# Expert feed-forward blocks: weights stationary, tokens moving, unrolled blocks

## The reference, cut to what matters

```python
logits = x @ router_w + router_b                 # x: layer-normed tokens, 2048 x 256; 8 experts
top_v, top_i = jax.lax.top_k(softmax(logits), 2)
weights = zeros((T, E)).at[arange(T)[:, None], top_i].set(top_v / sum(top_v))
gate = einsum('td,edi->eti', x, gate_w) + gate_b[:, None, :]      # i: 512 FF units
up   = einsum('td,edi->eti', x, up_w) + up_b[:, None, :]
h = silu(gate) * up
expert_out = einsum('eti,eid->etd', h, down_w) + down_b[:, None, :]
y = einsum('te,etd->td', weights, expert_out)                     # then t + y
```

## Time and profile before

| | us |
|---|---|
| median of three runs | 454.5 |
| span of the profiled execution, first to last instruction | 453.7 |
| runs, lowest and highest | 454.16, 454.62 |
| PE, DVE, POOL, ACT busy | 346.5, 343.3, 288.8, 209.2 |
| expert stage, first to last issue of L1146 (`weigh`) | 254.2 to 444.1 |

### The profile page before, as it was taken

How to read it: one execution, slowest core, us unless ns; L and a number is a source line. 1 busy time by engine, 2 the same in 40 slices (tenths; PEclk the granted TensorE clock), 3 DMA queues, 4 the chain that set the end, 5 groups by cost and what they waited for, 6 DMA issues and landing times.

```text
span 453.7 us, 13159 instructions
## 1 busy us (share of the span) xinstructions
PE 346.5 (76%) x4491; PEld 214.4 (47%) x4492; DVE 343.3 (76%) x693; ACT 209.2 (46%) x343; POOL 288.8 (64%) x459
## 2 busy tenths in 40 slices
PE   0078677767866766697259998999999999999971
PEld 0077434444444454542023654656566566565540
DVE  6988799799899999877882776666776776677650
ACT  1047637755956857645501433334434434433430
POOL 5616456666666666644585367777877878788651
PEclk9997568668668668689569999999999999999995
DMA  8410002322322222507764132333233333323322
GB/s 197 123 36 1 2 2 96 95 94 97 95 92 92 92 95 94 144 2 194 219 248 139 25 48 46 48 56 58 46 56 55 51 49 55 58 46 58 56 25 23
DMA packets 24960, 35.27 MB, mean 78 GB/s; under 512 B 4992, under 2 KB 18304, under 8 KB 24160
## 3 DMA queue, kind: packets, MB, share of 16 engines
q1 hardware_dynamic: 16256, 24.46, 17.5%
q0 software_dynamic: 7488, 10.23, 14.1%
q10 hardware_dynamic: 1184, 0.14, 0.2%
HBM read 25.39 MB, written 9.44 MB: 77 GB/s over the span
## 4 chain that ended last, share of the span: by engine, by line
PE 25%; DVE 23%; issue 19%; POOL 13%; DMA 9%; ACT 5%; DVEq 2%; POOLq 1%; SPq 1%; ACTq 0%
PE bank L881 6%; DMA w_stage<-token_rows,q_hi 5%; POOL w_stage L513 4%; PE bank L902 3%; POOL small L509 3%; DVE att L1348 2%; PE bank L549 2%; DVE s_exp L1314 2%; DVE v_exp L1367 2%; PE bank L777 2%; DVE q_exp L1382 2%; POOL v_exp L488 2%; PE bank L664 2%; DVE maxes L1307 2%; DMA token_rows<-z_stack 1%
## 5 line engine op out<-in xcount | busy, mean ns | idle before, releaser
L881 PE MATMUL bank<-w_exp,w_stage 128*128 x468 | 113.7, 380 | 1.3 <-issue 0.2
L526 POOL DMA_INDIRECT out_dram<-w_stage,q_hi x39 | 62.4, 1600 | 16.9 <-issue 16.9
L881 PEld LDWEIGHTS bank<-w_exp,w_stage 128*128 128x128 f16 x468 | 45.6, 97 | 41.8 <-issue 4.6
L408 POOL TENSOR_TENSOR w_exp<-w_stage,w_exp 128x1024 f16<-128x1024 f32 (+1 forms) x24 | 51.0, 2129 | 22.4 <-ACT w_exp L1041 22.4
L902 PE MATMUL bank<-w_exp,q_exp 128*128 x468 | 58.6, 276 | 2.1 <-DVE q_exp L1587 2.1
L513 POOL DMA_INDIRECT w_stage<-token_rows,q_hi x39 | 48.1, 1234 | 6.0 <-issue 6.0
L1570 DVE TENSOR_TENSOR v_exp<-bank,x_rows 128x512 f32<-128x512 f32 x39 | 27.0, 692 | 32.9 <-PE bank L881 32.8
L1146 ACT ACTIVATE w_stage<-w_stage,gate 128x256 f32<-128x256 f32 x39 | 19.8, 508 | 68.2 <-DVE w_stage L1592 68.2
L902 PEld LDWEIGHTS bank<-w_exp,q_exp 128*128 128x128 f16 x468 | 43.0, 98 | 11.8 <-issue 5.4
L1127 ACT ACTIVATE w_stage<-bank 128x256 f16<-128x256 f32 x39 | 14.9, 383 | 52.9 <-PE bank L869 52.9
L1587 DVE TENSOR_TENSOR q_exp<-bank,q_exp 128x512 f16<-128x512 f32 x39 | 27.0, 692 | 10.2 <-ACT q_exp L1138 10.0
(11 more groups left out here) (253 smaller groups left out, 814.2 us busy)
## 6 DMA issues: line engine op xcount, KB each, us to landing
w_stage<-in_L_ffn_gate_w_dram SPq DMA_DIRECT2D x8, 512.0 KB, 3.5
w_stage<-in_L_ffn_up_w_dram SPq DMA_DIRECT2D x8, 512.0 KB, 3.5
w_stage<-in_L_ffn_down_w_dram SPq DMA_DIRECT2D x8, 512.0 KB, 3.5
x_rows<-in_x_dram SPq DMA_DIRECT2D x8, 256.0 KB, 6.1
out_dram<-x_rows SPq DMA_DIRECT2D x4, 512.0 KB, 6.0
token_rows<-z_stack SPq DMA_DIRECT2D x4, 512.0 KB, 6.0
x_rows<-in_L_ffn_gate_b_dram SPq DMA_DIRECT2D x1, 2048.0 KB, 11.6
z_stack<-in_L_ffn_up_b_dram SPq DMA_DIRECT2D x2, 1024.0 KB, 6.8
```

What stands on the lines that cost most here:

```text
L408: pool.tensor_tensor(lo, w_stage[:, k, :], hi, ALU.subtract).then_inc(s["w_lo_done"], 1)
L526: pool.indirect_dma_start(out, bass.IndirectOffsetOnAxis(s_idx[par], 0), yw[par], None, compute_op=ALU.add).then_inc(s["y_scattered"], 16)
L881: mm = pe.matmul(GU[par][k][:], xs[par][:, c, :], w_exp[:, w * W_EXP + k * W_PIECE + c * FF:][:, bass.ds(e, FF)], start=(n == 0), stop=(n ...
```

## The change

`hidden` swaps its operands: for each of 4 chunks of 128 FF units and 2 chunks of channels, a 128x128 piece of `w_exp` is stationary and the 128 tokens move, 24 matmuls for gate and 24 for up. The result has FF units on partitions, which is the layout `down` needs, so `hidden_turned` goes. The biases become one value per partition in a new tile `b_cols`, filled in the first stage by two small DMAs, one transpose on TensorE and one copy on VectorE; the 4 MB broadcast loads go. `silu` takes the gate bias inside the activation, straight from PSUM, in four pieces of 128 columns; `gated` adds the up bias and multiplies in one instruction for each of four pieces. All blocks are written out instead of looped. GpSimd uses the table columns as index operands, without copies and holds, and the order of gathers and scatters, of the two hidden halves, and of the work on VectorE and ScalarE is as below.

```diff
-                pool.tensor_copy(g_idx[par], t_gather[:, bass.ds(b, 1)]).then_inc(s["gcol_ready"], 1)
-                pool.wait_ge(s["gcol_ready"], b + 1)
-                pool.tensor_tensor(hold[1], one_word, one_word, ALU.mult)
-                pool.indirect_dma_start(xg[par], None, token_rows, bass.IndirectOffsetOnAxis(g_idx[par], 0))\
+            def gather(b):
+                if b >= 2:
                     pool.wait_ge(s["xt_ps"], b - 1)
+                pool.indirect_dma_start(xg[b % 2], None, token_rows,
+                                        bass.IndirectOffsetOnAxis(t_gather[:, b:b + 1], 0))\
+                    .then_inc(s[f"x_got{b % 2}"], 16)
+            def scatter(b):
+                if b >= 1:
                     pool.wait_ge(s["y_scattered"], 16 * b)
                 pool.wait_ge(s["y_ready"], b + 1)
...
-            gather(0, 0, first=True)
-            gather(0, 1, first=True)
-            gather(1, 0)
-            gather(1, 1)
-            scatter(0, 0, first=True)
-            with pool.Fori(0, 2 * BODY - 1) as i:
-                gather(i + 2, 0)
-                scatter(2 * i + 1, 1)
-                gather(i + 2, 1)
-                scatter(2 * i + 2, 0)
+            gather(0)
+            gather(1)
+            for b in range(BLOCKS):
+                if b + 2 < BLOCKS:
+                    gather(b + 2)
+                scatter(b)
...
-                for xs, w in ((x_hi, 0), (x_hi, 1), (x_lo, 0)):
+                for f in range(FF_CHUNKS):
                     for c in range(2):
-                        mm = pe.matmul(GU[par][k][:], xs[par][:, c, :],
-                                       w_exp[:, w * W_EXP + k * W_PIECE + c * FF:][:, bass.ds(e, FF)],
-                                       start=(n == 0), stop=(n == 5))
+                        for xs, w in ((x_hi, 0), (x_lo, 0), (x_hi, 1)):
+                            mm = pe.matmul(GU[b % 2][k][:, P * f:P * f + P],
+                                           w_exp[:, w * W_EXP + k * W_PIECE + c * FF + P * f:][:, bass.ds(e, P)],
+                                           xs[b % 2][:, c, :], start=(c == 0 and xs is x_hi and w == 0),
+                                           stop=(c == 1 and w == 1))
...
+            for b in range(BLOCKS):                  # TensorE
+                if b + 1 < BLOCKS:
+                    e = weights_of(b + 1)
+                    hidden(b + 1, 0, e)
+                    hidden(b + 1, 1, e)
+                e = weights_of(b)
+                if b + 2 < BLOCKS:
+                    load_expert(b + 2)
+                    tokens_in(b + 2)
+                down(b, e)
...
+            for b in range(BLOCKS):                  # ScalarE
+                if b >= 1:
+                    weigh(b - 1)
+                if b + 1 < BLOCKS:
+                    silu(b + 1)
+                if b + 2 < BLOCKS:
+                    tokens_high(b + 2)
+                if b + 1 < BLOCKS:
+                    hidden_high(b + 1)
...
+            for b in range(BLOCKS):                  # VectorE
+                if b >= 1:
+                    down_bias(b - 1)
+                if b + 1 < BLOCKS:
+                    gated(b + 1)
+                if b + 2 < BLOCKS:
+                    tokens_low(b + 2)
+                if b + 1 < BLOCKS:
+                    hidden_low(b + 1)
```

More of the change, by code:

```diff
@@ L895, in down @@
-            def down(b, par, e, first=False):
+                        for xs, w in ((x_hi, 0), (x_lo, 0), (x_hi, 1)):
[3 more added lines that the diff above has]
+                                           stop=(c == 1 and w == 1))
+                mm.then_inc(s["gate_ps"] if k == 0 else s["up_ps"], 1)
@@ L896, in down @@
+            def down(b, e):
                 pe.wait_ge(s["hl_ready"], b + 1)
-                if not first:
+                if b >= 1:
                     pe.wait_ge(s["yadd_ready"], b)
                 n = 0
-                for c in range(4):
+                for c in range(FF_CHUNKS):
                     for hs, w in ((h_hi, 0), (h_lo, 0), (h_hi, 1)):
-                        mm = pe.matmul(YB[:, 0:L_COL], hs[par][:, c, :],
+                        mm = pe.matmul(YB[:, 0:L_COL], hs[b % 2][:, c, :],
@@ L906, in down @@
                 mm.then_inc(s["y_ps"], 1)
[L908 to L921, removed]
             pe.wait_ge(s["tables_ready"], 1)
-            load_expert(0, 0)
-            load_expert(1, 1)
-            tokens_in(0, 0, first=True)
+            load_expert(0)
+            load_expert(1)
+            tokens_in(0)
             keep_warm(4)
[L928 to L939, removed]
+            e = weights_of(0)
+            hidden(0, 0, e)
+            tokens_in(1)
+            hidden(0, 1, e)
+            for b in range(BLOCKS):
[8 more added lines that the diff above has]
+                down(b, e)
         @block.scalar
@@ L1128, in tokens_high, with silu @@
                                ACT.Copy).then_inc(s["xh_ready"], 1)
-            def silu(b, par, first=False):
-                act.wait_ge(s["gadd_ready"], b + 1)
-                if not first:
-                    act.wait_ge(s["h_ready"], b - 1)
-                act.activation(g_silu[par], g_sum[par], ACT.Silu).then_inc(s["silu_ready"], 1)
-            def hidden_high(b, par, first=False):
-                act.wait_ge(s["ht_ps"], b + 1)
-                act.activation(h_hi[par], bank[5][:].rearrange("p (c t) -> p c t", c=4),
+            def silu(b):
+                e = act.value_load(t_expert[0:1, b:b + 1], min_val=0, max_val=EXPERTS - 1)
+                if b >= 2:
+                    act.wait_ge(s["h_ready"], FF_CHUNKS * (b - 1))
+                act.wait_ge(s["gate_ps"], b + 1)
+                for f in range(FF_CHUNKS):
+                    act.activation(g_silu[b % 2][:, P * f:P * f + P], bank[2 * (b % 2)][:, P * f:P * f + P], ACT.Silu,
+                                   bias=b_cols[:, bass.ds(e * FF_CHUNKS + f, 1)]).then_inc(s["silu_ready"], 1)
@@ L1139, in hidden_high, with weigh @@
+            def hidden_high(b):
+                act.wait_ge(s["h_ready"], FF_CHUNKS * (b + 1))
+                if b >= 2:
+                    act.wait_ge(s["y_ps"], b - 1)
+                act.activation(h_hi[b % 2], h_sb[b % 2].rearrange("p (c t) -> p c t", c=FF_CHUNKS),
                                ACT.Copy).then_inc(s["hh_ready"], 1)
-            def weigh(b, par, first=False):
+            def weigh(b):
                 act.wait_ge(s["yadd_ready"], b + 1)
-                if not first:
-                    act.wait_ge(s["scol_ready"], b)
-                act.activation(yw[par], y_sum[par], ACT.Copy, scale=t_weight[:, bass.ds(b, 1)])\
+                if b >= 2:
+                    act.wait_ge(s["y_scattered"], 16 * (b - 1))
+                act.activation(yw[b % 2], y_sum[b % 2], ACT.Copy, scale=t_weight[:, b:b + 1])\
@@ L1147, in weigh @@
                     .then_inc(s["y_ready"], 1)
-            def act_block(b, par, first=False, more=2):
-                hidden_high(b, par, first=first)
-                if more >= 1:
-                    silu(b + 1, 1 - par, first=first)
-                if more >= 2:
-                    tokens_high(b + 2, par)
-                weigh(b, par, first=first)
-            tokens_high(0, 0, first=True)
-            tokens_high(1, 1, first=True)
-            silu(0, 0, first=True)
-            act_block(0, 0, first=True)
@@ L1161, in _ @@
-            with act.Fori(0, BODY) as i:
-                for k in range(4):
-                    act_block(4 * i + k + 1, (k + 1) % 2)
-            act_block(BLOCKS - 2, 1, more=1)
-            act_block(BLOCKS - 1, 0, more=0)
+            tokens_high(0)
+            silu(0)
+            tokens_high(1)
+            hidden_high(0)
+            for b in range(BLOCKS):
+                if b >= 1:
+                    weigh(b - 1)
[5 more added lines that the diff above has]
+                    hidden_high(b + 1)
@@ L1168, in _ @@
+            weigh(BLOCKS - 1)
         @block.vector
@@ L1586, in hidden_low, with down_bias @@
+            def hidden_low(b):
                 dve.wait_ge(s["hh_ready"], b + 1)
[L1587 removed]
+                if b >= 2:
+                    dve.wait_ge(s["y_ps"], b - 1)
+                dve.tensor_tensor(h_lo[b % 2], h_sb[b % 2].rearrange("p (c t) -> p c t", c=FF_CHUNKS), h_hi[b % 2],
                                   ALU.subtract).then_inc(s["hl_ready"], 1)
[L1590 removed]
+            def down_bias(b):
+                e = expert_of(b)
@@ L1608, in _ @@
-            tokens_low(0, 0)
-            tokens_low(1, 1)
-            e0 = expert_of(0)
-            dve.wait_ge(s["bias_rows"], 32)
-            gate_bias(0, 0, e0, first=True)
-            dve.wait_ge(s["up_rows"], 32)
-            up_bias(0, 0, e0)
-            gated(0, 0, first=True)
-            dve_block(0, 0, first=True)
-            with dve.Fori(0, BODY) as i:
-                for k in range(4):
-                    dve_block(4 * i + k + 1, (k + 1) % 2)
```

(11 more changed lines are left out.)

150 lines of the change are left out of this document (48 added, 102 removed).

## The result

The kernel after takes 631.72 us (median of 4 runs, 630.16 to 632.44), the kernel before beside it 454.56 us (4 runs): a ratio of 1.390, 95% interval 1.387 to 1.393, slower. Forecast were 612 us, and 568 to 644.

What follows compares the result with a forecast made beforehand. The bound was taken to be a circle of waits for one block through gather and scatter: 0.5 + 1.7 + 3.5 + 2.4 + 1.0 = 9.1 us, 9.4 with cold downs; 36 rounds plus head and tail gave 612 us, range 568 to 644.

Steps and rivals of the forecast that it cites:

- The step that carried it: GpSimd's queue: gather b+2 stands behind scatter b-1, which waits for down(b-1), so rounds go from 5.01 to 9.4 us.
- circle for one block: Down(b-1), weigh, scatter b-1, gather b+2, token transposes, down(b) wait on each other in turn: 9.1 us warm, 9.9 cold.
- a: End of weigh to start of the scatter: 0.83 us before, taken 0.5 without the hold, bounds 0.3 and 0.83.
- b: Start of scatter to start of gather: 2.27 us before, taken 1.7 without copy and hold, bounds 1.6 and 2.27.
- c: Start of gather to start of the token transposes, landing included: taken 3.5 us, bounds 2.8 and 3.9.
- d: Start of the token transposes to start of down_bias: taken 2.4 us warm, 3.2 cold, bounds 2.04 and 3.3.
- e: Start of down_bias to end of weigh: 1.08 us before, taken 1.0, bounds 0.95 and 1.08.
- the mechanism: TensorE's clock falls in the round's pause of about 3 us; some 4 in 10 downs run cold, round 9.4 us.
- My first rival: Gather on time, TensorE's sequencer bounds: 40 register operations at 0.12 us plus about 1.0, round 5.9, total 487 us; chance 0.09.
- P: The time of one round of the expert stage, the circle's length: taken 9.4 us, from 8.2 to 10.3.
- Edits taken at nothing: Edits around the rounds, such as small bias loads, dropping the 4 MB of broadcasts and unrolled code: each taken as 0.
- The forecast rival of 436 us: Faster than before: TensorE's array bounds the round at 4.5 us, total 436 us; chance 0.06.

Runs made afterwards that it cites:

- e1: The kernel after with one edit: GpSimd issues gather b+3 ahead of scatter b again, as before the change; 505.66 us, 1.116 of before.
- e2: The kernel before with one edit: scatter b stands ahead of gather b+3, holds and copies kept; 646.12 us, 1.427 of before.
- e4: As e1, but TensorE reads expert 0's weights at a fixed address for every block, without address operations; 451.65 us, 0.997 of before.
- e3: The kernel after with six unused 512-column matmuls between hidden and the token transposes of each round; 604.36 us.
- e5: The kernel before with table columns as indices, no copies or holds, GpSimd's blocks written out, gather b+3 still ahead of scatter b; 447.92 us, 0.988 of before.
- e6: As e1, but only down reads expert 0's weights at a fixed address, 8 register operations fewer; 506.86 us, 1.118 of before.
- e7: As e1, but only the gate half of hidden reads expert 0's weights at a fixed address, 16 operations fewer; 456.41 us, 1.004 of before.
- e8: As e5, without the 4 MB of broadcast bias loads, so the additions read other data; 448.79 us, 0.986 of before.

## Why the prediction was right

**The step that carried it held.** That gather b+2 now stands behind scatter b-1, and that this makes a circle for one block, is shown from both sides: e1 takes it out of the new kernel (-126 us), e2 puts it into the old one (+193 us). It is shown without the operands, the layout or the unrolling, so the swapped matmuls are not what the 177 us are mainly about. The 51 us that e1 leaves are about the price of the addresses: e4 takes 54 us off e1.

**The terms of the round.** Means over the 36 rounds of the profile after, beside the forecast (warm is a round at 2.4 GHz, cold one at 1.2):

| term | forecast | measured | |
|---|---|---|---|
| a, weigh to scatter | 0.5 | 0.80 | the hold went, but 0.75 of "issue" stayed |
| b, scatter to gather | 1.7 | 1.89 | 1.59 and 0.30 |
| c, gather to token transposes | 3.5 | 3.08 | the landing fell from 3.2 to 2.8 |
| d, transposes to down_bias | 2.4 warm, 3.2 cold; 2.72 mixed | 3.00 | from 2.2 (warm) to 3.4 (cold) |
| e, down_bias to the end of weigh | 1.0 | 0.97 | |
| round | 9.4 | 9.73 | 12 us in 36 rounds |

Three terms came out longer than forecast (a by 0.30, b by 0.19, d by 0.28) and c shorter by 0.42. The sum is off by 0.34 only because these partly cancel, which is luck. Why the landing fell is not isolated; it is 2.8 in the three kernels with the circle for one block (after, e2, e3) and 2.9 to 3.2 in those with the gather ahead (before, e1, e5, e6, e7). In a, I took away the hold's 0.18 and a part of the pause behind it; the pause was not the hold's. Where the scatter waits for `weigh`, a measures 0.80 in every kernel here without the hold, against 0.83 to 0.85 with it (before, e2), so the hold was worth next to nothing there; what the direct columns saved lies in b (2.27 to 1.89).

**The clock.** I let 4 in 10 downs be cold, from two pauses of before. In the profile after, 28 of the first 37 lie above 2.6 us in term d, three in four, and the mean granted clock of the stage is 0.82. So the mechanism was right and its share was put too low. Behind a pause of 3.10 us the level was 0.50, that is 1.2 GHz (the stretch from 384.40 above); behind the 1.29 us that e3 leaves it was 2.4 GHz. The pauses run from 2.5 to 4.7 us, and the length of one pause does not say alone what the next down takes: in the timeline above, the one of 3.73 us was followed by a down of 1.84, the one of 2.71 by a down of 2.76. What decides within the round stays open. The Trainium skill ("TensorE: Matmul & The Clock Gate", Why this matters for your kernels) warns of idle gaps of about this length between bursts; as a warning this agrees with the trace, but not as a limit, since here the cold down came behind the shorter pause. e3 gives the price in this kernel, 27 us.

**TensorE's sequencer.** The trace of before showed the operations 0.12 us apart, and hidden was put at 4.0 us. The spacing holds: its median is 0.124 to 0.125 us in the kernels before and after and in every run here that has such operations. Hidden itself takes 2.9 to 4.4 us in the kernel after, 3.7 on average, and as forecast costs nothing there, as it is covered by the pause. My first rival (487 us if the gather were on time) came within 19 us of the 505.7 of e1, but partly by luck: it adds down's 8 operations to hidden's 32, and e6 shows that down's cost nothing, while the rest of the round beside hidden's operations is 2.2 us and not 1.0. Two traces show how it goes. First e1, one round (L1509 is `tokens_low`, for whose result the next hidden waits):

```profile
355.89 0.41 PE L836 MATMUL bank<-ident,w_stage 128*128 128x128 f32 x2 [0.35 <-issue]
356.23 1.48 PE L861 MATMUL bank<-w_exp,q_exp 128*128 x12
356.92 0.42 DVE L1509 TENSOR_TENSOR w_stage<-bank,w_stage 128x256 f16<-128x256 f32 x1
357.54 4.26 PE L848 MATMUL bank<-w_stage,w_exp 128*128 128x128 f16 x48
```

In 34 rounds of e1 the first address operation of hidden came 0.04 to 0.11 us behind the end of L1509. So the operations stand behind hidden's wait for the new tokens, and the 1.45 us from the start of the transposes to the end of L1509 are spent whatever down does: down's operations and matmuls lie beside them. The round of e1 is these 1.45 us, the 32 operations of 4.1 us, and some 0.7 from the last of them to the next transposes. In the kernel after a cold down gives them a head start, because the tokens are ready before down ends:

```profile
316.30 0.42 DVE L1509 TENSOR_TENSOR w_stage<-bank,w_stage 128x256 f16<-128x256 f32 x1 [3.75 <-ACT w_stage L1073]
...
L848 PEldq FUSED_REGOPS  x32: 46/46/46, 316.8 to 320.9; - x32
...
318.20 3.06 PE L848 MATMUL bank<-w_stage,w_exp 128*128 128x128 f16 x48
```

Twelve of the 32 operations were issued before the first of these matmuls at 318.20, and hidden took 3.06 us.

**Head and tail.** The first weigh came at 259.9 instead of the 255.4 forecast, after 254.2 before. 1.8 of it lies ahead of the expert stage: the first gather's index table is ready at 240.2 instead of 238.5. In e1, e3 and e4, which have the same first stages as the kernel after, it is ready at 238.6 to 238.9, so the edits to these stages cost at most 0.4; the rest belongs to the one execution that was profiled, and its cause is not shown. Another 1.8 is a wait that I had not seen: hidden(1) needs the low parts of token tile 1, which VectorE now makes behind gated(0). The last 0.9 has no account. The end, from the last weigh on, took 11.2 instead of 8.9: the last two blocks come 2.3 us apart, and the last scatter waits for the landing of the one before. The two rounds without gathers took 9.1, as forecast (9.2). Together: 12 (rounds) + 4.5 (head) + 2.3 (end) + 0.3 (the runs' median lies 1.1 above the span, not 0.8) = 19 us, the distance from 612.7 to the measured value. The bounds of the forecast follow from its own sum only to within 1.5 us (P of 8.2 to 10.3 gives 569.5 to 645.1, not 568 to 644); the measured value lies inside either.

**Edits taken at nothing** were right where tested: the 4 MB of loads (e8). What the transposes of h and the fused biases are worth, no run isolates. With all of the change's work savings, the good order and free addresses, e4 is at 0.997 of before; the old operands with GpSimd's part (e5) are at 0.988. So no gain from the new operands shows even then. The forecast rival of 436 us needed rounds of 4.5; e4 reaches 4.88, and waits for the gather again.

## What to carry to other kernels

When one engine issues, in order, both the fetch for a later block and the write-back of an earlier one, write down for each fetch which result it stands behind and in which round it is used: moving it by one place (e2) turned a circle for two blocks into one for a single block, and the length of the circle, read part by part from the chain of waits, gave the new time within 5%. When a dynamic address moves from the long operand to the short one, count distinct addresses, not matmuls: the columns stayed the same and the address work went from 16 to 40 operations a block.

## What the runs showed of the hardware

- A register operation for an operand's address takes 46 ns in its row, but the operations come 0.124 us apart (median). They stood behind hidden's wait for its tokens (0.04 to 0.14 us after the end of L1509 in e1 and the kernel after), and behind it ran ahead of the matmuls: by 12 operations in the round shown. 32 of them beside 2.85 us of matmuls made hidden 4.2 to 4.4 us long in e1; 16 of them cost it nothing (e7), and down's 8 cost nothing (e6).
- An indirect DMA on GpSimd came 0.80 us after the end of the ScalarE instruction that it waited for (0.75 of it "issue"), and 0.83 to 0.85 with a small instruction in between. Behind another DMA it came after 0.30 us where nothing stood in between (after), and after 0.67 with a copy and a hold (before, 427.57 to 428.24).
- Six unused matmuls per round made the kernel 27 us faster (e3): the granted clock of the stage rose from 0.82 to 0.98, and only the part of the round with the transposes and down got shorter.
